# Slot-routed feed-forward on one Trainium2 core: one set of logits turned into both softmaxes, sums by a column of ones

## The reference

```
xn  = rms_norm(x1) * gamma_x                      # 1024 x 128
se  = rms_norm(slot_embeds) * gamma_slot          # 512 slots x 128
logits   = xn @ se.T                              # 1024 tokens x 512 slots (8 experts x 64)
dispatch = softmax(logits, over the tokens)       # axis=1
slots    = dispatch.T @ xn                        # 512 x 128
h        = gelu(slots @ w1);  processed = h @ w2  # 512 x 512, then 512 x 128
combine  = softmax(logits, over the slots)        # axis=-1
out      = layernorm(x1 + combine @ processed)
```

## Time and profile before

| what | value |
|---|---|
| three runs | 1857.96, 1858.75, 1860.97 us |
| profiled execution | 1854.99 us, of it 1853.2 us span |
| attention, up to its last matmul | 1478 us |
| feed-forward, first load to the end | 1484.7 to 1853.2 us |
| busy in the span | PE 95%, PEld 81%, DVE 81%, ACT 67%, POOL 59% |
| granted TensorE clock, mean | 0.983 of 2.4 GHz |

### The profile page before, as it was taken

The page is one execution under the profiler, slowest core; times in us unless marked ns, Lnnn a source line. Parts: engine busy times, 40 slices in busy tenths (PEclk is TensorE's granted clock), DMA queues, the critical chain, the costliest instruction groups (busy, mean ns, idle before and its releaser), DMA issues. The chain is left out here.

```text
span 1853.2 us, 33608 instructions
## 1 busy us (share of the span) xinstructions
PE 1760.0 (95%) x10556; PEld 1501.7 (81%) x10556; DVE 1493.9 (81%) x2926; ACT 1242.0 (67%) x2450; POOL 1087.1 (59%) x661
## 2 busy tenths in 40 slices
PE   4899999999999999999999999999999859999997
PEld 3788888888888888878888888888888637888886
DVE  3789988887898878878988898899899667777774
ACT  2677777776777777767777777777777524555553
POOL 3556665665666666656665666666666333555444
PEclk7999999999999999999999999999999979999999
DMA  3223332233222222322332223222322130111100
GB/s 102 69 71 79 79 105 69 70 81 82 69 69 80 81 69 74 89 71 79 80 98 74 70 69 92 69 69 69 84 77 78 39 95 24 36 34 36 43 12 24
DMA packets 69767, 127.90 MB, mean 69 GB/s; under 512 B 15456, under 2 KB 42080, under 8 KB 69600
## 3 DMA queue, kind: packets, MB, share of 16 engines
q1 hardware_dynamic: 68416, 124.81, 24.6%
q10 hardware_dynamic: 1184, 1.05, 0.2%
HBM read 50.07 MB, written 8.65 MB: 32 GB/s over the span
## 5 line engine op out<-in xcount | busy, mean ns | idle before, releaser
L454 ACT ACTIVATE probs<-ps_slot,neg_max 128x640 f32<-128x640 f32 (+7 forms) x512 | 378.7, 741 | 124.6 <-DVE neg_max L540 115.1
L540 DVE CUSTOM_DVE_ANT_0 ps_slot<-ps_slot,causal 128x640 f32<-128x640 f32 (+7 forms) x512 | 387.1, 756 | 47.5 <-PE ps_slot L57 45.8
L691 PE MATMUL ps_turn<-ident,probs 128*128 128x128 f32 x2304 | 340.5, 277 | 18.9 <-DVE x_t L597 5.8
L691 PEld LDWEIGHTS ps_turn<-ident,probs 128*128 128x128 f32 x2304 | 256.1, 140 | 54.0 <-issue 8.1
L418 POOL TENSOR_TENSOR q<-rot_q,q 128x1024 fp32r<-128x1024 f32 x64 | 153.7, 2401 | 240.8 <-ACT q L471 240.8
L55 PE MATMUL ps_slot<-k,q 128*128 128x512 f32 (+3 forms) x768 | 282.9, 368 | 2.3 <-DVE rot_q L556 1.4
L57 PE MATMUL ps_slot<-k,q 128*128 128x512 f32 (+3 forms) x768 | 265.6, 346 | 0.0
L56 PE MATMUL ps_slot<-k,q 128*128 128x512 f32 (+3 forms) x768 | 265.6, 346 | 0.0
L410 POOL TENSOR_TENSOR swapped_q<-swapped_q,rope 128x1024 f32<-128x1024 f32 x64 | 164.5, 2570 | 79.2 <-DMA swapped_q<-unrot_q 78.9
L418 POOL TENSOR_TENSOR k<-rot_k,k 128x1024 fp32r<-128x1024 f32 x64 | 153.1, 2393 | 87.8 <-ACT k L471 86.7
L556 DVE TENSOR_TENSOR rot_q<-ps_slot,rope 128x1024 f32<-128x1024 f32 x64 | 78.4, 1225 | 137.7 <-ACT unrot_q L465 137.7
(11 more groups left out here) (165 smaller groups left out, 4491.4 us busy)
## 6 DMA issues: line engine op xcount, KB each, us to landing
swapped_k<-unrot_k SPq DMA_DIRECT2D x128, 256.0 KB, 3.6
swapped_q<-unrot_q SPq DMA_DIRECT2D x128, 256.0 KB, 3.7
inv_b<-inv_rows SPq DMA_DIRECT2D x64, 512.0 KB, 4.8
x_rows<-in_L_attn_x SPq DMA_DIRECT2D x8, 512.0 KB, 5.1
y_t<-y_sum SPq DMA_DIRECT2D x8, 512.0 KB, 5.2
y_in<-y_t SPq DMA_DIRECT2D x7, 512.0 KB, 3.4
x_row<-in_L_attn_x SPq DMA_DIRECT2D x7, 512.0 KB, 4.6
out<-out_row SPq DMA_DIRECT2D x7, 512.0 KB, 3.2
```

Source lines behind the costliest of these rows:

```text
L454: act.activation(probs_tile(t), score_tile(name, head, i), ACT.Exp, scale=-1.0, bias=neg_max[:, head.par, t:t + 1], accum_out=sums[:, head ...
L540: dve.tensor_tensor_reduce(tile, tile, causal[:, T - WIDTH[t]:T], -1.0, UNSEEN, ALU.add, ALU.min, neg_max[:, head.par, t:t + 1]).then_inc( ...
L691: last = pe.transpose(bank[:, at:at + P], probs_tile(t)[:, j * P:(j + 1) * P], ident[:, :])
```

## The change

`ffn_block` is rewritten; attention stays.

- The logits are made once, slots in the partitions (`find_logits`, 4 chunks of 6 products). VectorE finds each slot's maximum over the tokens (`find_peak`), ScalarE copies the chunk to SBUF with that maximum subtracted (`shift`, to `logits`).
- TensorE turns the shifted logits tile by tile (`turn_tile`, 8 tiles of four transposes, the columns taken with a step of four), ScalarE takes the exponential straight into `disp` (`weights_of_slots`). It is not scaled: `z_row` has a 129th column of ones, so `sum_slots` (now 4 products of 129 columns for each tile, `disp` stationary) gives the sums too, and `scale_slots` divides. The slot sums have the slots in the partitions then, and `turn_slots` turns them.
- For the softmax over the slots each token's maximum is needed. VectorE finds it from the turned tile in PSUM plus the slot maxima (`find_row_peak`), which it needs along the row in every partition: SP writes the 512 maxima to DRAM and reads them back into all partitions (`spread_peaks`, `peak_b`). The token maxima go the same way in two halves (`spread_rows`, `row_b`). GpSimd adds them to `logits` (`sub_rows`), ScalarE takes the exponential in place in `comb` (`weights_of_rows`). These weights too are unscaled; `proc` has a column of ones, and `add2` divides while it adds x1.
- The output of a batch is summed and added in the next batch in four quarters of two tiles (`sum_out(q)`, `add2(q)`). The product with w2 moves into the next batch (`sum_proc`), its copy from ScalarE to VectorE.
- The rows of x1 move from VectorE to GpSimd (`input_rows`). The split of the turned tokens is done in halves that put the tokens back in their order.
- At the start `se_raw` is loaded behind the first tokens, its squares are summed between the statistics of the two halves, and the first logits wait for both halves of `z_t`.

The diff, cut to its core:

```diff
-ROW_TILES = ((0,), (1,), (2,), (3,), (4, 5), (6, 7), (8, 9), (10, 11))
+z_row = [s.sb(f"z_row{i}", [P, NT, D1], F32) for i in range(2)]
+logits = [s.sb(f"logits{i}", [P, NC, T], F32) for i in range(2)]
...
+def tile_bank(t):
+    return ps_turn[:, (t + 1) % 2, :]
+def by_token(cols, t):
+    return cols.rearrange("q (p t) -> q t p", t=4)[:, t % 4, :]
...
+    def spread_peaks(b, par, first):
+        wait_apart(sp, peak_made, b + 1, sp_ticks)
+        sp.dma_start(c_rows[par, :].rearrange("(p c) -> p c", c=NC), peak[:, par, :])\
+          .then_inc(peak_stored, 16)
+        wait_apart(sp, peak_stored, b * 16 + 16, sp_ticks)
+        if not first:
+            wait_apart(sp, row_peaked, b * NT, sp_ticks)
+        sp.dma_start(peak_b[:, :], c_rows[par:par + 1, :].to_broadcast([P, N])).then_inc(peak_landed, 16)
...
+    def batch(b, par, first, stored, ahead):
+        spread_peaks(b, par, first)
+        if ahead:
+            wait_apart(sp, added1, b * 2 + 2, sp_ticks)
+            load(b + 2)
+        if stored:
+            store(b - 2)
+        for half in range(2):
+            spread_rows(b, par, half, first)
...
-    def norm_rows(b, i):
-        wait_apart(pool, inverted, b * 12 + i + 1, ticks)
-        _, row = row_tile(i, 0)
-        pool.tensor_scalar(row, row, inv[:, i:i + 1], 1.0, ALU.mult, ALU.mult).then_inc(normed, 1)
...
+    def sub_rows(b, par, half, first):
+        wait_apart(pool, row_landed[half], b * 16 + 16, ticks)
+        if not first:
+            wait_apart(pool, out_summed, b * 4 - 2 * (1 - half), ticks)
+        for c in range(NC):
+            pool.tensor_tensor(comb[:, c, half_cols(half)], logits[par][:, c, half_cols(half)],
+                               row_b[:, half, :], ALU.add).then_inc(subbed, 1)
...
         if ahead:
             wait_apart(pool, stats_b, b + 1, ticks)
             first_norm(base, norm1_known)
-        for i in range(8, 12):
-            norm_rows(b, i)
+        for half in range(2):
+            sub_rows(b, par, half, first)
+        if ahead:
+            input_rows(b + 1, 1 - par, first)
         if not first:
             second_norm(b - 1, base)
             output_rows(b - 1)
...
+    def shift(b, par, c):
+        act.wait_ge(peaked, b * NC + (c + 1))
+        act.activation(logits[par][:, c, :], slot(c), ACT.Identity,
+                       bias=neg_peak[:, par, c:c + 1]).then_inc(shifted, 1)
+    def weights_of_slots(b, t):
+        act.wait_ge(tile_turned, b * NT + (t + 1))
+        act.activation(disp[:, t, :], tile_bank(t), ACT.Exp).then_inc(disped, 1)
+    def weights_of_rows(b, par, half, chunks):
+        for c in chunks:
+            act.wait_ge(subbed, b * 2 * NC + (half * NC + c + 1))
+            act.activation(comb[:, c, half_cols(half)], comb[:, c, half_cols(half)], ACT.Exp,
+                           bias=peak[:, par, c:c + 1]).then_inc(combed, 1)
...
+    def batch(b, par, first, ahead):
+        if not first:
+            weights_of_rows(b - 1, 1 - par, 0, range(1))
+        shift(b, par, 0)
+        shift(b, par, 1)
+        if not first:
+            weights_of_rows(b - 1, 1 - par, 0, range(1, NC))
+        shift(b, par, 2)
+        shift(b, par, 3)
+        weights_of_slots(b, 0)
+        weights_of_slots(b, 1)
+        if not first:
+            weights_of_rows(b - 1, 1 - par, 1, range(NC))
+        for t in range(2, NT):
+            weights_of_slots(b, t)
         if ahead:
+            for half in range(2):
+                split_zt(half, z_turned, b * 2 + (half + 1), turn(f"z{half}"), zt_hi)
+        split_slot_in(b)
+        gelu(b, 0)
+        gelu(b, 1)
...
+    def find_row_peak(b, par, t):
+        wait_apart(dve, disped, b * NT + (t + 1), dve_ticks)
+        if t == 0:
+            wait_apart(dve, peak_landed, b * 16 + 16, dve_ticks)
+        tile = tile_bank(t).rearrange("q (c p) -> q p c", c=NC)
+        dve.tensor_tensor_reduce(tile, tile, peak_b[:, :].rearrange("q (p c) -> q p c", c=NC), -1.0, UNSEEN,
+                                 ALU.add, ALU.min, neg_row[:, par, t:t + 1]).then_inc(row_peaked, 1)
...
+    def add2(b, par, q):
+        dve.wait_ge(out_summed, b * 4 + (q + 1))
+        dve.wait_ge(x1_made, b + 1)
+        dve.wait_ge(out_made, b * NT + 1)
+        sums = out_bank(q)[:, 0:2 * D1].rearrange("p (t d) -> p t d", d=D1)
+        dve.reciprocal(inv_out[:, 2 * q:2 * q + 2], sums[:, :, D]).then_inc(out_inverted, 1)
+        dve.wait_ge(out_inverted, b * 4 + (q + 1))
+        for i in range(2):
+            t = 2 * q + i
+            last = dve.scalar_tensor_tensor(res2[:, t, :], sums[:, i, 0:D], inv_out[:, t:t + 1],
+                                            x1[par][:, t, :], ALU.mult, ALU.add)
+        last.then_inc(added2, 1)
...
+        row_stats(res, 0, None, half + 1, first_stats_a, first_stats_b, tiles)
+        if half == 0:
+            dve.wait_ge(se_landed, 16)
+            for c in range(NC):
+                dve.tensor_tensor_reduce(se_sq[:, c, :], se_raw[:, c, :], se_raw[:, c, :], 1.0, 0.0,
+                                         ALU.mult, ALU.add, rms[:, c:c + 1]).then_inc(setup, 1)
...
+        for c in range(NC):
+            find_peak(b, par, c)
+        turn_peaks(b, par)
+        if not first:
+            copy_proc(b - 1)
...
+        find_row_peak(b, par, 0)
+        find_row_peak(b, par, 1)
+        if not first:
+            add2(b - 1, 1 - par, 0)
+            add2(b - 1, 1 - par, 1)
+        find_row_peak(b, par, 2)
+        find_row_peak(b, par, 3)
+        find_row_peak(b, par, 4)
         if ahead:
             dve.wait_ge(norm1_known, b + 1)
             scale_rows(1 - par, half_tiles(0))
+        find_row_peak(b, par, 5)
         if ahead:
             scale_rows(1 - par, half_tiles(1)).then_inc(z_made, 1)
+        find_row_peak(b, par, 6)
+        find_row_peak(b, par, 7)
+        scale_slots(b)
         if ahead:
+            for half in range(2):
+                split_zt(half, zt_hi, b * 2 + (half + 1), turn(f"z{half}"), zt_lo)
+        if not first:
+            add2(b - 1, 1 - par, 2)
+        split_slot_in(b)
+        if not first:
+            add2(b - 1, 1 - par, 3)
+            dve.wait_ge(added2, b * 4)
+            row_stats(res2, 1, None, b, stats2_a, stats2_b)
...
+    def find_logits(c):
+        own = slice(c * P, (c + 1) * P)
+        for half in range(2):
+            last = matmul_split(pe, slot(c)[:, half_cols(half)], se_t[:, 0, own], se_t[:, 1, own],
+                                z_t[:, 0, half_cols(half)], z_t[:, 1, half_cols(half)], True, True)
+        last.then_inc(logits_in, 1)
+    def turn_tile(b, par, t):
+        if t >= 2:
+            pe.wait_ge(row_peaked, b * NT + (t - 1))
+        for c in range(NC):
+            last = pe.transpose(tile_bank(t)[:, c * P:(c + 1) * P],
+                                by_token(logits[par][:, c, half_cols(t // 4)], t), ident[:, :])
+        last.then_inc(tile_turned, 1)
+    def sum_slots(b, par, t):
+        pe.wait_ge(disped, b * NT + (t + 1))
+        for c in range(NC):
+            last = pe.matmul(slot_sum(c), disp[:, t, c * P:(c + 1) * P], z_row[par][:, t, :],
+                             start=t == 0 and c % 2 == 0, stop=t == NT - 1, skip_group_check=True)
         return last
...
+    def sum_out(q):
+        for i in range(2):
+            t = 2 * q + i
+            for c in range(NC):
+                last = pe.matmul(out_bank(q)[:, i * D1:(i + 1) * D1],
+                                 by_token(comb[:, c, half_cols(q // 2)], t), proc[:, c, :],
+                                 start=c == 0, stop=c == NC - 1)
+        last.then_inc(out_summed, 1)
...
             pe.wait_ge(first_added, 2)
+            pe.wait_ge(first_lo, 2)
...
+        find_logits(1)
+        if not first:
+            sum_proc((0, 1))
+        pe.wait_ge(shifted, b * NC + 1)
+        find_logits(2)
+        pe.wait_ge(shifted, b * NC + 2)
+        find_logits(3)
+        if not first:
+            sum_proc((2, 3)).then_inc(proc_summed, 1)
         if ahead:
             pe.wait_ge(in_landed, b * 32 + 32)
+            token_transposes(0, turn("tok0"), tokens_turned)
+        if not first:
+            pe.wait_ge(proc_copied, b)
...
+            pe.wait_ge(added1, b * 2 + 1)
+        pe.wait_ge(shifted, b * NC + NC)
+        turn_tile(b, par, 0)
+        if ahead:
+            pe.wait_ge(added1, b * 2 + 2)
+        turn_tile(b, par, 1)
+        if not first:
+            pe.wait_ge(combed, b * 2 * NC - NC)
+            sum_out(0)
+            sum_out(1)
+        sum_slots(b, par, 0)
+        sum_slots(b, par, 1)
+        turn_tile(b, par, 2)
+        for t in range(3, NT):
+            turn_tile(b, par, t)
+            sum_slots(b, par, t - 1)
+        sum_slots(b, par, NT - 1).then_inc(slots_summed, 1)
+        if ahead:
+            pe.wait_ge(z_made, b + 1)
+            pe.wait_ge(row_peaked, b * NT + 7)
+            z_transposes(1 - par, 0, turn("z0"), z_turned)
+            pe.wait_ge(row_peaked, b * NT + 8)
```

(37 more changed lines are left out.)

491 lines of the change are left out of this document (170 added, 321 removed).

## The result

The changed kernel took 1881.63 us, the median of 4 runs from 1878.56 to 1883.27, beside 1858.76 for the kernel before on the same chip: a ratio of 1.0122, 95% interval 1.0108 to 1.0135. Forecast were 1832 us and a range from 1808 to 1857. The profiled execution has a span of 1876.5 us for 1853.2.

A forecast was written before the change was run, and what follows sets the result against it. TensorE, busy 49.65 of 50 us, was taken as the bound. Six batches falling from 41.43 to 37.7 us gave 22.4, plus 2 (start) plus 3 (last batch) less 1 (tail), 26.4 us: 1832 us against the median, range 1808 to 1857.

The forecast's parts named there:

- stationary side of the output product: Output product reading `comb` with a step of four: 0.9 us a batch, 0.014 for each of 64 instructions.
- upper bound of 2.7 us a batch: Output product: load growing by the transpose's 71 ns, spacing in proportion, from 0.116 to 0.159 us an instruction.
- Rival 3: Strided operands on VectorE and TensorE cost double: peaks 1.22 us, splits 1.2, weights 1.8 more; 44.9 a batch, 1884 us; chance 0.12.
- TensorE's work: Steady batch if TensorE never waited: 41.4 us less 9.1 plus 1.4 leaves 33.7 us.
- hand schedule: One steady batch laid out from the previous last gelu across engines: 36.8 us, TensorE waiting 3 us, mainly for VectorE.
- Rival 1: TensorE-bound: waits overlap and strided weights cost nothing; a batch of 33.7 to 35.5 us, kernel 1812 us; chance 0.17.
- Rival 2: Maxima's transfers through DRAM come late: first peak at 16.5 instead of 14 us, 39.7 a batch, 1846 us; chance 0.16.
- Three terms of the ends: Start and end: first logits about 1510.4, batch 1 gaining 2 us; last batch 3 us gained; tail 1 us lost.
- GpSimd's 1.2 us a sum: GpSimd's sums for the token softmax: 8 of 512 a batch at 1.2 us each, 9.6 us.
- `shift` at 1.0: ScalarE's copy of a logits chunk less its maximum: about 1.0 us each, four a batch.
- the exponential: ScalarE's exponentials: 0.7 us in the tile loop, 16 a batch taking 9.6 us.
- Granted clock at 1.00: TensorE in the steady feed-forward: busy some 90% with its clock at 1.00, the upper level of 2.4 GHz.

The follow-up runs named there:

- experiment 1: Changed kernel with GpSimd writing `comb` tile by tile, so the output product reads it without a step; transposes keep theirs: 1821.12 us, ratio to before 0.9812.
- experiment 4: Kernel before with one edit: `comb` written with a step of four, so its output product reads its stationary operand with that step: 1921.01 us, 1.0346.
- experiment 7: Kernel before with `z_row` laid out with a step of four, loaded under slot sums of 512 columns and read so by its transposes: 1857.51 us, 0.9999.
- experiments 5 and 6: Kernel before with `comb` written and read by the output product with a step of two, then of eight: 1861.54 us (1.0011) and 1925.23 us (1.0367).
- version 2: Changed kernel with no step anywhere on TensorE: `comb`, `z_t` and the logits lie in tile order: 1820.57 us, 0.9809.
- version 8: version 2 with TensorE's wait for VectorE's low half of `z_t` moved behind output quarter 2: 1811.57 us, 0.9756.
- version 9: version 8 with the next batch's loads and the store issued behind the maxima's way out and back: 1828.32 us, 0.9841.

## Why the prediction was wrong

**The failed step** is the one on the stationary side of the output product: "I take 0.9, as the nearest row is the strided transpose: 0.014 each", with an upper bound of 2.7 us a batch. It measured 7.6 (experiment 1). Even the row it leans on says more: 0.024 for each strided transpose is 1.5 us for 64. The sum of the other steps holds: 1832 less the 0.9 put down in each of six batches is 1826.6, and the kernel without the step took 1821.1. With the 60.5 us of experiment 1 in place of that 5.4 the sum gives 1887, for 1881.6 measured.

Two things were wrong in it. The bound let the load grow by as much as the transpose's, 71 ns; it grew by 137. And the spacing was taken to grow in proportion to the load, from 0.116 by 263 / 192; with 329 for 263 that rule would give 0.199, and 0.233 was measured. Measured from start to start, the contiguous product's instructions are 0.112 us apart (3.57 us for 32; the prediction's 0.116 is a group's length divided by 64) and the stepped ones 0.233. Loads of 192 ns at 0.112 overlap their neighbour by 80 ns, loads of 329 at 0.233 by 96. The spacing rose by 0.121 us in the changed kernel and by 0.118 in experiment 4, the load by 0.137, so nearly all that was added came through. At 512 columns none came through (experiment 7).

A hint stood in the rows: the product's loads kept PEld busy for 59.4 us, and the product itself lasted 8 x 7.41 = 59.3, so a longer load had no idle time to use. By itself this was no proof. The transposes' loads also follow one another without a gap in the kernel before (8 in 0.92 us, from 1645.45), and of the 67 ns by which theirs grew, 141 to 208, only 0.024 us came through. The step adds less to a transpose's load even on the same operand: in experiment 7 `z_row` loads take 211 ns for 151 as the transposes' operand and 309 for 189 as the product's. Why that is so, and why less of it comes through, no run here shows.

**The rule behind it.** The Trainium skill (SBUF — State Buffer, Door 1: The DMA port swizzle, on cachelines) has full rate only where an access finds a second hit in its 16 bytes. The runs agree with it, on the stationary load: step two (two numbers in 16 bytes) 196 ns, steps four and eight 329 and 334. The writes of VectorE and ScalarE into `comb` have their step at the same place (experiments 5 and 6). I had cited the rule and then took the price from the lower end.

**Rival 3 by name, not by its ground.** "Strided operands cost double, slower" gave 1884 and 0.12, and the time fell there by luck. Its main part was VectorE at 1.22 us a peak; that is 0.706 (forecast 0.69), and the splits, 1.2 us of it, take 0.681 on VectorE with the step in PSUM and without it (version 2). Its 2.7 for the weights was too small by 4.9. What cost double was the product: 0.233 for 0.112.

**Point by point.**
- TensorE's work 33.7 us a batch: right, 34.0 in version 8.
- The hand schedule 36.8 without the strided weights: near, 35.4 in version 2. Its last peak ended 24.8 us after the last gelu (1645.45 less 1620.64) for 26.9 forecast. In the changed kernel it was 29.0 (1662.61 less 1633.57), as the first two quarters of output took 7.46 us for 3.7.
- Rival 1, TensorE-bound, 1812 and 0.17: that is version 8, once the step and one wait are gone (1811.6). The middle of its 33.7 to 35.5 is 34.6 and not 34.8, which moves its time by 1 us.
- Rival 2, the first peak at 16.5: it came at 15.5, late as feared, and the time didn't go by it.
- Three terms of the ends: the first logits were forecast near 1510.4 and came at 1508.54, with attention over 1.5 us sooner (1476.41 for 1477.88). Batch 1 gained 1.3 for 2, but by two misses that nearly cancel: batch 0 began 1.9 us sooner than forecast and took 36.4 us for 34. The last batch's 3 us were eaten by its output product, and the tail lost 7.4 for 1, of which 15.20 - 7.41 = 7.8 is the product again.
- GpSimd's 1.2 us a sum (1.28), `shift` at 1.0 (1.11), the exponential: right.
- "Granted clock at 1.00": nearly; 0.97 in the stretch above. Busy time by stage of the changed kernel, two parts of a batch:

```profile
1644.60:1652.10 7.50, 7.50 (x34) 7.50 (x34) 3.78 (x21) 3.05 (x5) 4.30 (x8) 1.00 1.02 227
...
1664.90:1673.30 8.40, 8.38 (x37) 8.38 (x37) 2.09 (x5) 1.97 (x2) 2.89 (x3) 0.80 0.12 31
```

Behind a pause of TensorE ahead of 1664.92 the granted clock is 0.80, a mean between the levels of 1.2 and 2.4 GHz. It costs nothing in the output product: the two quarters take 3.90 and 3.57 us there (1664.92 to 1668.82, 1669.67 to 1673.24), 0.233 for each of 32 instructions, as at 1.00. The stepped load takes 329 ns at 0.59 (1667.0 to 1668.8) as at 1.00. A contiguous one doesn't keep its time: in version 9 it takes 333 ns at 0.50 (1635.3 to 1638.0) for 192. That fits a rate set by the load, with a stepped load that does not follow the clock.

## What to carry to other kernels

Before an operand's layout is changed, look at what TensorE loads as stationary: with float32 numbers 16 bytes or more apart, and 128 columns to stream, each instruction took twice its time, and that turned a gain of 36 us (version 1) into a loss of 23. Under 512 columns the same step cost nothing. Let an engine with time to spare write the tiles contiguous; here GpSimd did it at no cost. When the range hangs on one price that no row shows, a neighbour's price is no guide: here a transpose's 0.024 us stood for a product's 0.118, and one edit of the kernel before (experiment 4) would have measured it.

## What the runs showed that I had not expected

- The cost of a stepped stationary load is a stair, not a slope: 196 ns at a step of two, 329 at four, 334 at eight, 192 contiguous; whole kernel 1.0011, 1.0346, 1.0367.
- The stepped load and the spacing of its products don't follow TensorE's granted clock: 329 ns at 0.59 and at 1.00, 0.233 us at 0.80 and at 1.00. A contiguous load does: 192 ns at 1.00 and 333 at 0.50.
- VectorE and ScalarE read PSUM with a step of 128 numbers at full rate: 0.706 us for a peak of 512, and for the splits of `z_t` 0.681 and 0.594 us with the step, 0.681 and 0.595 without (version 2).
- Writing 512 numbers into SBUF with a step of four is another matter: 1.112 us for 0.606 on ScalarE, 1.071 for 0.680 on VectorE; with a step of two 0.641 and 0.681.
- A 2 KB store queued behind 1.5 MB of loads and stores on SP's queue held up its read back for 7.1 us, for 1.5 without (experiment 9).
